# Routing tokens to expert regions inside the attention loop, and running the experts block by block

## What is computed

```python
h = tok(x)                                  # [64, 197, 192]
h = h + attn(layernorm(h))                  # 12 heads of 16; q and k normalised per head
x2 = layernorm(h).reshape(12608, 192)
scores = sigmoid(x2 @ gate_weight.T)        # 8 experts in 4 groups of 2
s = scores + gate_bias
# the two groups with the largest sums, in them the two largest s
w = scores[chosen]; w = w / (w.sum() + 1e-6)
y = sum over the chosen e:  w_e * (silu(x2 @ w1[e].T) * (x2 @ w3[e].T)) @ w2[e].T    # 192 -> 128 -> 192
z = (silu(x2 @ sw1.T) * (x2 @ sw3.T)) @ sw2.T                                       # shared expert
return h + y + z
```

## Time and profile before

| | us |
|---|---|
| median of 3 runs (2129.76 to 2136.05) | 2130.58 |
| the profiled execution | 2126.83 |
| its span in the trace | 2124.9 |
| PE busy, share of span | 1922.6, 90% |
| DVE busy | 1320.9, 62% |
| ACT busy | 908.2, 43% |
| POOL busy | 42.2, 2% |
| mean granted TensorE clock | 0.984 of full |
| bytes moved | 74.83 MB |

### The profile page before, as it was taken

One profiled execution on the slowest core, in us unless ns is written; L12 is line 12 of the kernel. 1 busy time (PEld: TensorE's weight loads), 2 busy tenths in 40 slices (PEclk: granted clock), 3 DMA queues, 4 the chain that ended last, 5 costly groups with the idle time before them and its releaser, 6 DMA issues. The chain is left out here.

```text
span 2124.9 us, 48134 instructions
## 1 busy us (share of the span) xinstructions
PE 1922.6 (90%) x17848; PEld 1351.2 (64%) x17848; DVE 1320.9 (62%) x3554; ACT 908.2 (43%) x1878; POOL 42.2 (2%) x63
## 2 busy tenths in 40 slices
PE   3999989899899898998998699999999999999998
PEld 3777767677677776776776355555555555555556
DVE  3444444444344444444444488788888888888888
ACT  2555545455455555555555233333333333333332
POOL 0000000000000000000000000000000000000000
PEclk9999999999999999999999799999999999999999
DMA  4011111111111111111110000000000000000000
GB/s 146 16 45 44 48 43 45 46 44 45 46 45 44 46 44 46 45 45 46 44 44 10 32 16 30 17 21 23 15 30 15 22 22 15 30 15 30 16 21 13
DMA packets 31517, 74.83 MB, mean 35 GB/s; under 512 B 3435, under 2 KB 16366, under 8 KB 31214
## 3 DMA queue, kind: packets, MB, share of 16 engines
q1 hardware_dynamic: 31310, 72.10, 10.8%
...
## 5 line engine op out<-in xcount | busy, mean ns | idle before, releaser
L571 ACT ACTIVATE prob<-ps_sc 99x792 f32<-99x792 f32 x384 | 317.5, 827 | 256.0 <-PE ps_sc L413 256.0
L357 PE MATMUL ps_hid<-lin_f,xin 128*99 128x192 f32 x1536 | 289.9, 333 | 65.7 <-DVE v L684 36.1
L905 PE MATMUL ps_h<-yT_hi,w_hi 96*128 96x512 f16 (+1 forms) x900 | 342.8, 381 | 0.0
L907 PE MATMUL ps_h<-yT_lo,w_hi 96*128 96x512 f16 (+1 forms) x900 | 341.3, 379 | 0.0
L908 PE MATMUL ps_h<-yT_hi,w_lo 96*128 96x512 f16 (+1 forms) x900 | 340.9, 379 | 0.0
L357 PEld LDWEIGHTS ps_hid<-lin_f,xin 128*99 128x99 f32 x1536 | 240.3, 169 | 77.0 <-issue 47.2
L979 ACT ACTIVATE in_hi<-inner 128x512 f16<-128x512 f32 (+1 forms) x225 | 140.3, 624 | 338.3 <-DVE inner L1098 338.3
L923 PE MATMUL ps_y<-w_hi,in_hi 128*128 128x192 f16 (+1 forms) x900 | 222.4, 247 | 40.6 <-DVE acc L1122 29.0
L971 ACT ACTIVATE act<-ps_h 128x512 f32<-128x512 f32 (+1 forms) x225 | 132.3, 588 | 278.6 <-PE ps_h L908 277.9
L1122 DVE SCALAR_TENSOR_TENSOR acc<-ps_y,comb,acc 128x192 f32<-128x192 f32 (+1 forms) x700 | 242.3, 407 | 0.0
L1098 DVE SCALAR_TENSOR_TENSOR inner<-ps_h,act 128x512 f32<-128x512 f32 (+1 forms) x225 | 152.7, 679 | 130.0 <-ACT act L971 119.8
...
## 6 DMA issues: line engine op xcount, KB each, us to landing
...
hin<-hidden_dram SPq DMA_DIRECT2D x24, 384.0 KB, 3.0
out<-acc SPq DMA_DIRECT2D x24, 384.0 KB, 2.3
...
hidden_dram<-h SPq DMA_DIRECT2D x64, 0.8 KB
...
```

Of the source, the lines that this page charges most:

```text
L357: last = pe.matmul(hid[:, t, :], xin[q][:, k, t * TR:(t + 1) * TR], lin_f[:, k, :], start=(k == 0), stop=(k == PCHUNKS - 1))
L571: act.activation(prob[quad][:, places].rearrange("p h m s -> p h (m s)"), ps_sc[0:TR, places, 0:2 * SLOTS], ACT.Exp, scale=D ** -0.5 / (SQ ...
L905: pe.matmul(bank[:, 0:N], w13_hi[:, k, e, w, :], yT_hi[p][:, k, 0:N], start=(k == 0), stop=False)
L907: pe.matmul(bank[:, 0:N], w13_hi[:, k, e, w, :], yT_lo[p][:, k, 0:N], start=False, stop=False)
```

## The change

Stage one also routes. After the residual of image k-5, DVE takes the statistics of h2 (`h2_stats_of`); one step later the normalised row is made (`rows_out`), PE transposes it (`turn`) and multiplies by the gate (`gate`, f32), and the sigmoid is made from Exp. `route` finds in three parts the two chosen experts and their weights. PE products with a triangle of ones (`places`) count the tokens per expert ahead of each token, `place_out` adds the running count, and POOL scatters each token's row of 196 values (192 features, weight, token number) twice with indirect DMAs to the chosen experts' regions of `dispatch` in device memory. The shared expert is computed here as well, in f32 (`shared_inner`, `shared_sigmoid`, `shared_gate`, `shared_outer`); `base_add` adds it to h2, and SP stores that sum to `out`. 16 steps are written out ahead of the loop, and 8 behind it.

Stage two reads the counts, fills the open end of each region with rows that have a token number out of range, and makes a table (`make_table`) of 208 entries: expert, offset, and how many earlier adds must have landed. Then 205 blocks of 128 rows run, in loops of 8: SP loads a block from the offset in the table, PE transposes it and multiplies by that expert's weights (their addresses from a register), ACT scales by the row's weight, and POOL adds the 128 rows to `out` with an indirect DMA that accumulates. An add waits for the add two blocks before, and for the last one where the expert is a new one.

```diff
+CHOICES = 2
+BLOCK = 128
+ROW = C + 4
+W_AT, ID_AT = C, C + 1
+CAP = TOTAL + BLOCK
+SLOTS_D = EXPERTS * CAP + BLOCK
+BLOCKS = CHOICES * TOTAL // BLOCK + EXPERTS
+TABLE = BLOCKS + 3
+NOWHERE = 1 << 20
+XB = 8
...
+            def gate(n, attended):
+                pe.wait_ge(yT_set, n.times(1, 1))
+                if attended.active():
+                    pe.wait_ge(oT_out, attended.times(QUADS, 3))
+                for t in range(2):
+                    for k in range(2):
+                        last = pe.matmul(gate_ps[:, t, :], yT[:, k, t * TR:(t + 1) * TR], gate_f[:, k, :],
+                                         start=(k == 0), stop=(k == 1))
+                last.then_inc(gate_done, 1)
...
+                pe.matmul(place_ps[:, 0, :], bef99[here, :], first, start=True, stop=True)
+                pe.matmul(place_ps[:, 1, :], ones99[here, :], first, start=True, stop=False)
+                pe.matmul(place_ps[:, 1, :], bef99[:], second, start=False, stop=True)
+                pe.matmul(all_ps, ones99[here, :], first, start=True, stop=False)
+                pe.matmul(all_ps, ones99[:], second, start=False, stop=True).then_inc(place_done, 1)
...
+                for w in range(2):
+                    for k in range(2):
+                        last = pe.matmul(s_h[w], w13_f[:, k, EXPERTS, w, :], yT[:, k, :],
+                                         start=(k == 0), stop=(k == 1))
...
                 if n3.active():
                     transpose_qk(n3, 1, 0)
+                if n6.active():
+                    turn(n6, n4)
                 if n2.active():
                     qk(n2, 0)
+                if n7.active():
+                    shared_outer(n7, n4)
                 if n3.active():
                     transpose_qk(n3, 1, 1)
                 if n1.active():
                     embed(n1, 2)
                 if n3.active():
+                    if n7.active():
+                        pe.wait_ge(base_done, n7.times(1, 1))
                     scores(n3, 0)
                 if n5.active():
                     pe.wait_ge(onorm_done, n5.times(2, 2))
...
+                if n7.active():
+                    places(n7, n4, n6)
+                if n6.active():
+                    gate(n6, n4)
+                if n6.active():
+                    shared_inner(n6, n1)
...
-                    attend(n3, 0)
+                    attend(n3, 0, None, n6, n7)
...
-                    values(n2, n1)
+                    values(n2, n1, n6)
...
+            def shared_sigmoid(n):
+                act.wait_ge(s_h_done, n.times(1, 1))
+                act.activation(s_exp[:], s_h[0], ACT.Exp, scale=-1.0).then_inc(sexp_done, 1)
+                act.wait_ge(sexp_done, n.times(1, 1))
+                act.activation(s_ln[:], s_exp[:], ACT.Ln, bias=ones[0:INTER]).then_inc(sln_done, 1)
+                act.wait_ge(sln_done, n.times(1, 1))
+                if reached(n.times(1)):
+                    act.wait_ge(ssilu_done, n.times(1))
+                act.activation(s_sig[:], s_ln[:], ACT.Exp, scale=-1.0).then_inc(ssig_done, 1)
...
+            def rows_out(n):
+                q = n.mod(4)
+                dve.wait_ge(h2rstd_done, n.times(1, 1))
+                if reached(n.quarters(SCATTERS)):
+                    dve.wait_ge(scattered[q], n.quarters(SCATTERS))
+                for t in range(2):
+                    last = dve.tensor_scalar(rows[q][:, t, 0, 0:C], h2[q][:, t, :], h2_mv[:, t, 0:1],
+                                             h2_rstd[:, t:t + 1], ALU.subtract, ALU.mult)
+                last.then_inc(rows_done, 1)
...
+                def then(ins):
+                    step_no[0] += 1
+                    ins.then_inc(route_step, 1)
+                    dve.wait_ge(route_step, n.times(ROUTE_STEPS, step_no[0]))
+                def ranks(values, gap, over, far, rank, M):
+                    of_j = values[:].unsqueeze(2).broadcast_to([TR, 2, M, M])
+                    of_i = values[:].unsqueeze(3).broadcast_to([TR, 2, M, M])
+                    then(dve.tensor_tensor(gap[:], of_j, of_i, ALU.subtract))
+                    then(dve.tensor_tensor(over[:].rearrange("p t i j -> p t (i j)"),
+                                           gap[:].rearrange("p t i j -> p t (i j)"),
+                                           far[:].rearrange("p i j -> p (i j)").unsqueeze(1)
+                                           .broadcast_to([TR, 2, M * M]), ALU.is_gt))
+                    then(dve.tensor_reduce(rank[:].rearrange("p t i -> p (t i)"),
+                                           over[:].rearrange("p t i j -> p (t i) j"), AX.X, ALU.add))
...
+                    dve.wait_ge(gexp_done, n.times(1, 1))
+                    then(dve.tensor_scalar(gden[:], gexp[:], 1.0, None, ALU.add))
+                    then(dve.reciprocal(score[:], gden[:]))
+                    then(dve.tensor_tensor(biased[:], score[:], gbias[:], ALU.add))
+                    pairs = biased[:].rearrange("p t (g two) -> p t g two", two=2)
+                    then(dve.tensor_tensor(gsum[:], pairs[:, :, :, 0], pairs[:, :, :, 1], ALU.add))
+                    ranks(gsum, gap4, over4, far4, rank4, EGROUPS)
...
+                    then(dve.tensor_scalar(drop4[:], rank4[:], 1.5, -FAR, ALU.is_gt, ALU.mult))
+                    by_two = drop4[:].rearrange("p t g -> p (t g)").unsqueeze(2).broadcast_to([TR, 2 * EGROUPS, 2])
+                    then(dve.tensor_tensor(masked[:].rearrange("p t (g two) -> p (t g) two", two=2),
+                                           biased[:].rearrange("p t (g two) -> p (t g) two", two=2),
+                                           by_two, ALU.add))
+                    ranks(masked, gap8, over8, far8, rank8, EXPERTS)
+                if part_no == 2:
+                    if reached(n.times(1)):
+                        dve.wait_ge(place_done, n.times(1))
+                    dve.tensor_scalar(taken[:], rank8[:], 1.5, None, ALU.is_lt).then_inc(taken_done, 1)
+                    then(dve.tensor_tensor(pick[:], by_choice(rank8), choice_no[:], ALU.is_equal))
+                    then(dve.tensor_tensor(wpick[:], pick[:], by_choice(score), ALU.mult))
+                    then(dve.tensor_reduce(wsel[:], wpick[:], AX.X, ALU.add))
+                    then(dve.tensor_reduce(wsum[:], wsel[:], AX.X, ALU.add))
+                    then(dve.tensor_scalar(wden[:], wsum[:], 1e-6, SA * SW, ALU.add, ALU.mult))
+                    then(dve.reciprocal(wrec[:], wden[:]))
+                    dve.tensor_tensor(rows[n.mod(4)][:, :, :, W_AT], wsel[:],
+                                      wrec[:].unsqueeze(2).broadcast_to([TR, 2, CHOICES]),
+                                      ALU.mult).then_inc(weight_done, 1)
...
+            def place_out(n, gated):
+                dve.wait_ge(place_done, n.times(1, 1))
+                if gated.active():
+                    dve.wait_ge(gexp_done, gated.times(1, 1))
+                dve.wait_ge(weight_done, n.times(1, 1))
+                dve.tensor_tensor(place[:], place_ps, count[:].unsqueeze(1).broadcast_to([TR, 2, EXPERTS]),
+                                  ALU.add).then_inc(place_step, 1)
+                dve.wait_ge(place_step, n.times(2, 1))
+                dve.tensor_tensor(count[:], all_ps, count[:], ALU.add).then_inc(place_read, 1)
+                dve.tensor_tensor(at[:], pick[:], place[:].unsqueeze(2).broadcast_to([TR, 2, CHOICES, EXPERTS]),
+                                  ALU.mult).then_inc(place_step, 1)
+                dve.wait_ge(place_step, n.times(2, 2))
+                dve.wait_ge(place_read, n.times(1, 1))
+                if reached(n.times(1)):
+                    dve.wait_ge(slot_int, n.times(1))
+                dve.tensor_reduce(slot_f[:], at[:], AX.X, ALU.add).then_inc(slot_done, 1)
...
+            def shared_gate(n):
+                dve.wait_ge(ssig_done, n.times(1, 1))
+                dve.tensor_tensor(s_silu[:], s_h[0], s_sig[:], ALU.mult).then_inc(ssilu_done, 1)
+                dve.wait_ge(ssilu_done, n.times(1, 1))
+                if reached(n.times(1)):
+                    dve.wait_ge(s_y_done, n.times(1))
+                dve.tensor_tensor(s_in[:], s_h[1], s_silu[:], ALU.mult).then_inc(sin_done, 1)
...
             def step(k):
-                n1, n2, n3, n4, n5 = (k.back(d) for d in (1, 2, 3, 4, 5))
+                n1, n2, n3, n4, n5, n6, n7 = (k.back(d) for d in (1, 2, 3, 4, 5, 6, 7))
                 if n5.active():
                     o_out(n5, 1)
+                if n6.active():
+                    rows_out(n6)
                 if n3.active():
                     kT_copy(n3, 0)
                 if n2.active():
                     xT_out(n2)
+                if n7.active():
+                    route(n7, 1)
                 if n2.active():
                     qk_variance(n2, 0)
+                if n7.active():
+                    base_add(n7)
                 if n3.active():
                     kT_copy(n3, 1)
```

(96 more changed lines are left out.)

851 lines of the change are left out of this document (447 added, 404 removed).

## The result

The changed kernel takes 2244.9 us (median of 4 runs, 2235.1 to 2258.8) against 2131.0 before: ratio 1.053, 95% interval 1.047 to 1.060. It is 5.3% slower, where 3.4% faster was forecast. The profiled execution took 2258.8 us, with a span of 2257.0. It is the longest of the four, 14 us above their median, so a difference between its trace and that of another kernel can be that much too large.

What follows compares the result with a forecast made beforehand. DVE was to pace the attention loop, the scatter-adds the block stage. Set-up 26, loop 1385, turnover 33, blocks 605, last landing 4 made a span of 2053; plus 1.9 and 3.8 that gave 2059 us, range 1880 to 2290.

Steps and rivals of the forecast that it cites:

- The attention loop: Stage one with routing: 57 full steps of 21.3 us and 171 us of partial ones, 1385 us, +224.
- the scatter-adds: Block stage: one issue plus one landing, 5.7 us, spans two blocks and sets the pace, period 2.85 us.
- Register reads: Block stage: PE reads two registers per block, 0.3 us each, hidden under the period of 2.85 us.
- rival 4: Block stage: register loads bind PE from 0.95 us each; at 1.3 us each, 2274 us in all; chance 0.05.
- Rival 1: Block stage: scatter-adds slower than 3.30 us a block, from issue plus landing of 6.4 us; 2254 at 3.9; chance 0.24.
- Rival 2: Block stage: adds are quick; handing on between engines or PE with registers binds, period 2.1, 1885 us; chance 0.26.
- Rival 5: Block stage: PE at half clock, period about 3.2 us, 2109 us in all; counted with the forecast, no separate chance.
- PE per step: Attention loop: PE gets 1.8 us more per image, 18.3 us of work per step, staying below DVE.
- DVE per step: Attention loop: 8.64 us added, 17.0 us of DVE work; with waits it sets the pace at 20.6 us a step.
- Turns and stalls: Attention loop: the loop's turns add 0.6 us a step on the mean, as before the change.
- Partial steps: Attention loop: 15 steps without all parts, at the start and while draining, 171 us together.
- Rival 3: Attention loop: DVE's order, with new waits in series, drags the step to 24 us, 2213 in all; chance 0.08.

Runs made afterwards that it cites:

- b_once: Changed kernel with TensorE reading a block's expert once and keeping the register for the outer products in six of eight blocks: 2131.0 us.
- c_plain: Changed kernel, both stages written out, one register read per block, later scatters, new ACT and DVE order, block-stage DMAs writing without adding: 1950.7 us.
- b_static: Changed kernel with TensorE taking expert 0's weights at a fixed address in every block, its two register reads left out: 2071.3 us.
- b_plain: Changed kernel with the block stage's 205 indirect DMAs writing their rows and not adding them: 2258.8 us.
- b_warm: Changed kernel with filler products on PE, 80 ahead of the block stage and four in each block: 2246.0 us.
- a_order_noscat: Changed kernel, gate_exp after qk_rstds(n2, 1), residual(n5) before shared_gate(n6), loop scatters left out, block stage reading one empty block: 20.8 us a step, last store 1456.6.
- a_late: Changed kernel with POOL issuing an image's four scatters one step later, behind the copy of the next image's rows: 2223.7 us.
- a_straight: Changed kernel with the attention loop written out as 72 steps, no loop: 2174.1 us.
- c_straight_once: Changed kernel with attention loop and block stage both written out and each block's expert read once by TensorE: 2015.5 us, ratio to before 0.946.

## Why the prediction was wrong, step by step

The forecast failed in two of its terms. The attention loop was put at 1385 us and took 157 more; that alone makes the kernel slower than before, and without it the forecast's 2059 would have become some 2106, still faster. The expert stage was near in length (+42) by luck: the bound named, the scatter-adds, was put too high, and the real one, PE's stream with its register reads, too low.

**Register reads.** They were put at 0.3 us each and hidden under the scatter-adds. In the trace a read costs PE 0.86 to 1.0 us: TENSOR_LOAD 0.30, FUSED_REGOPS 0.15, SEQ_ASSERT 0.02, and the rest is the stretch in which no product is fed, until the waits behind it and the first product are through. b_once gives 0.67 for each read left out, with the adds' bound near, and c_plain 0.87. Two reads make 1.9 of 3.07 us. That is the mechanism of rival 4, to which 0.05 was given. Its time didn't come: its threshold of 0.95 each lies within what was measured, but the blocks stayed at 3.16 us, under the 3.30 of break-even. Its bounds (nothing to 3.0) held the price, and the value within them was taken because a read is a few bytes, which no row supported. The Trainium skill's 0.6 us (DMA: Bandwidth & Descriptors, Latency and other measured facts) lies above the 0.30 of the record and below the 0.86 that the block pays.

**The scatter-adds.** Forecast 5.7 us for issue plus landing, period 2.85; measured 4.4 and 2.2, once they bind (b_static). Two in flight was right. The issue was put at 0.4 and is 1.56, the upper end of its bounds; the landing was put at 5.3, and 4.4 leaves 2.5 for it when the issue and the gap of 0.30 ahead of it are taken off. As the bound of the changed kernel they were wrong: in b_plain their cost falls and nothing moves. Rival 1, which needed 6.4, fails with that. Rival 2 was right that the adds are quicker than forecast, and c_plain, at 2.25 with PE in the chain, comes near its 2.1; in the changed kernel the two reads stand in the way.

**The half clock.** Rival 5 had the period, 3.2, and the clock, 0.50, and the wrong cause: b_warm has 1.00 and the same time. A number that comes out right is no proof of its mechanism.

**Blocks in sum**: 644 us from the first add to the last, 3.16 each, of which the turns are 0.09; forecast 605. This is 42 of the 204 us.

**The attention loop** is the greater part, +157. Of these, 118 lie between the first store and the 57th (56 steps at 23.40 and not 21.3) and 46 behind the 57th; 7 were gained ahead of the first. Of the 2.1 us a step, 0.95 is the steady step (21.65 against 20.7, the forecast without its 0.6 for turns), and 1.2 is turns and stalls:
- *PE per step*: 18.3 forecast, 19.62 measured. The row "eight of 192 take 1.31 us" counts instructions; four of the program's float32 products make eight. The six new float32 products of the shared expert were so priced at half (1.0 us; their rows begin at 767.35 and 780.94 and take 1.52 and 0.66 to the next). The nine of 8 columns, put at 0.5, take 0.92: 0.22 for the five of places and 0.70 for the gate's four. PE, and not DVE, is the fuller engine.
- *DVE per step*: 17.0 forecast, 14.78 measured; small operations lie closer than 0.22 us where they don't depend on each other. The waits took it back: that for qk_rstd grew from 0.64 to 1.65 us, and 0.88 for s_sig is new. The sum 20.6 came near 21.65 with both parts wrong, which is luck. The forecast named gate_exp's place on ACT and gave it 0.1 (21.2 to 21.3), and it let the wait for qk_rstd stay as it was; the new order of ACT and DVE was worth 0.8 (a_order_noscat).
- *Turns and stalls*: 0.6 us a step forecast, 1.8 measured (23.40 - 21.6). Taken away in the order of a_late, 0.8 is the scatters' (23.40 - 22.60; less by the medians) and about 1.0 the turns', 10 us each where before had 3.0. The two don't simply add: written out, with the scatters in place, the loop has 21.81 (a_straight) and 21.63 (c_straight_once), so that hardly anything is left for the scatters. The forecast priced the scatters only as POOL's time (1.3 to 6.2 us; 4 x 0.99 was right) and never asked which of the other engines their rows would meet.
- *Partial steps*: 171 forecast; behind the 57th store alone 131 us pass to the end of the loop against 85, since the draining steps take 17 to 22 us and not 13. The clock isn't the reason for the first of them: it is 0.97 in 1500 to 1520 us and 0.50 in 1520 to 1540. No run takes this part by itself.
- *Rival 3* had 24 us a step and 2213 in all, near 23.40, by DVE's waits in series. Order was worth only 0.8 of the step; its number came near by other causes.

**The turnover** was right: table 18.1 us against 19.4, 38 us in all against 33. **POOL** and **SP** were hidden as said.

**Of the signs named as right**, PE near 85% busy in the loop came (87%), stores 20.5 to 21.5 us apart nearly came (21.65), DVE over 80% busy there (68%), PE under 60% busy in the block stage (81%) and POOL waiting for its own adds did not. The sign named as wrong, PE's sequencer in front of the block stage's products, is what the trace shows.
